# Attention of a two-layer kernel: weighted sum ahead of the row-minimum products, transposes back ahead of the output projection

## What is computed

```python
x = x + attention0(layernorm(x), ctx)      # rope on q and k
x = x + experts0(layernorm(x))             # top 2 of 8 experts + a shared one
x = x + attention1(layernorm(x), ctx)      # key mask, no rope
x = x + experts1(layernorm(x))             # top 4 of 16 experts + a shared one
# attention:
q, k, v = heads(x @ Wq.T + bq), heads(ctx @ Wk.T + bk), heads(ctx @ Wv.T + bv)
scores = einsum('bhsd,bhtd->bhst', q, k) / sqrt(16)
out = einsum('bhst,bhtd->bhsd', softmax(scores), v)
return out.reshape(B, S, 256) @ Wo.T + bo
```

## Time and profile before

| what | us |
|---|---|
| median of 3 runs | 952.73 (952.24 to 957.65) |
| profiled execution, time | 950.79 |
| profiled execution, span | 948.9 |
| TensorE busy | 868.0 (91% of the span) |
| VectorE busy | 650.6 (69%) |
| ScalarE busy | 483.4 (51%) |
| POOL busy | 383.0 (40%) |

### The profile page before, as it was taken

One profiled execution on the slowest core, in us unless ns is written; L12 is line 12 of the kernel. 1 busy time (PEld: TensorE's weight loads), 2 busy tenths in 40 slices (PEclk: granted clock), 3 DMA queues, 4 the chain that ended last, 5 costly groups with the idle time before them and its releaser, 6 DMA issues.

```text
span 948.9 us, 21025 instructions
## 1 busy us (share of the span) xinstructions
PE 868.0 (91%) x7941; PEld 763.1 (80%) x7941; DVE 650.6 (69%) x1364; ACT 483.4 (51%) x811; POOL 383.0 (40%) x389
## 2 busy tenths in 40 slices
PE   5689988889899999999777999899999999999997
PEld 4577766678899999999666788667788888888886
DVE  6868686675577777777575557559867666676676
ACT  3665669533367767676465665963222223223222
POOL 4354445057468888888513232301121131311210
PEclk9799999999999999999988999999999999999999
DMA  7019020014778888888530000100001010010002
GB/s 215 24 35 261 11 74 2 1 68 151 266 234 224 232 239 221 241 215 228 106 127 25 2 2 4 52 15 18 17 18 33 17 33 17 17 33 17 17 1 89
DMA packets 46176, 85.43 MB, mean 90 GB/s; under 512 B 6304, under 2 KB 33184, under 8 KB 45984
## 3 DMA queue, kind: packets, MB, share of 16 engines
q0 software_dynamic: 14784, 46.44, 17.8%
q1 hardware_dynamic: 31328, 38.09, 13.5%
HBM read 63.73 MB, written 20.79 MB: 89 GB/s over the span
## 4 chain that ended last, share of the span: by engine, by line
PE 64%; DVE 11%; ACT 9%; issue 6%; DMA 5%; POOL 4%; SPq 0%; DVEq 0%; ACTq 0%; POOLq 0%
PE bank L1430 35%; PE bank L1466 12%; PE bank L1525 4%; DMA w_raw<-in_fw,w_idx 2%; PE bank L1639 2%; ACT prob L760 2%; PE bank L1615 2%; PE bank L1689 2%; DVE low_f L1252 2%; PE bank L1723 2%; POOL summed L497 2%; DMA xs<-sorted_x 1%; DVE xres L1120 1%; PE bank L1699 1%; DVE xT_lo L943 1%
## 5 line engine op out<-in xcount | busy, mean ns | idle before, releaser
L1430 PE MATMUL bank<-xT_hi,w_hi 128*128 128x512 f32 x352 | 140.4, 399 | 2.8 <-DVE hid L1130 2.8
L691 ACT ACTIVATE act_sb<-bank 128x512 f32<-128x512 f32 x88 | 52.6, 598 | 172.3 <-PE bank L1430 172.3
L1430 PE MATMUL bank<-xT_lo,w_hi 128*128 128x512 f32 x352 | 140.1, 398 | 0.0
L1430 PE MATMUL bank<-xT_hi,w_lo 128*128 128x512 f32 x352 | 139.9, 397 | 0.0
L1130 DVE TENSOR_TENSOR hid<-bank,act_sb 128x512 f32<-128x512 f32 x88 | 60.9, 692 | 114.4 <-ACT act_sb L691 114.0
L1120 DVE SCALAR_TENSOR_TENSOR xres<-bank,gate,xres 128x256 f32<-128x256 f32 x320 | 132.6, 476 | 0.8 <-PE bank L1466 0.8
L427 POOL TENSOR_TENSOR w_hi<-w_raw,zero_col 128x768 fp32r<-128x768 f32 (+1 forms) x20 | 31.9, 1595 | 245.3 <-PE bank L1466 240.6
L1430 PE MATMUL bank<-xsT_hi,w_hi 128*128 128x256 f32 x368 | 106.4, 289 | 2.1 <-DVE xsT_lo L1094 1.5
L497 POOL DMA_INDIRECT summed<-y_sb,tile_to x46 | 96.4, 2096 | 25.2 <-issue 15.4
L1466 PE MATMUL bank<-w_hi,hid_hi 128*128 128x256 f32 x352 | 100.1, 284 | 5.8 <-DVE hid_lo L1135 5.8
L1430 PE MATMUL bank<-xsT_hi,w_lo 128*128 128x256 f32 x368 | 103.5, 281 | 0.0
(11 more groups left out here) (210 smaller groups left out, 2192.1 us busy)
## 6 DMA issues: line engine op xcount, KB each, us to landing
w_raw<-in_fw SPq DMA_DIRECT2D x18, 384.0 KB, 3.0
sorted_x<-empty_row SPq DMA_DIRECT2D x2, 2967.0 KB, 19.8
xs<-sorted_x SPq DMA_DIRECT2D x23, 258.0 KB, 3.3
ctx_raw<-in_ctxT SPq DMA_DIRECT2D x8, 512.0 KB, 4.5
xres<-in_x SPq DMA_DIRECT2D x4, 512.0 KB, 7.3
summed<-xres SPq DMA_DIRECT2D x4, 512.0 KB, 9.0
xres<-summed SPq DMA_DIRECT2D x4, 512.0 KB, 5.9
out_x<-xres SPq DMA_DIRECT2D x4, 512.0 KB, 3.0
```

Of the source, the lines that this page charges most:

```text
L691: nc.scalar.activation(act_sb[:, r, :], bank[2 * r + 1][:], ACT.Silu).then_inc(f["act"], 1)
L1430: last = nc.tensor.matmul(dst, lh, rh, start=(i == 0), stop=(i == len(pairs) - 1))
```

## The change

Three pairs of steps change places; no instruction's work is changed.

```diff
 # ScalarE, attend()
+                        if b >= 1:
+                            output_copy(b - 1)
                         exponential(b, 0)
                         exponential(b, 1)
-                        if b >= 1:
-                            output_copy(b - 1)
                         if b >= 2:
                             output_turned_copy(b - 2)
 # VectorE, attend()
+                        if b >= 1:
+                            output(b - 1)
                         if b >= 3:
                             residual(b - 3)
-                        if b >= 1:
-                            output(b - 1)
 # TensorE, attend()
                         if b >= 1:
                             scores_turned(b)
+                            weighed(b - 1)
                         lows_added(b)
                         if b == 0:
                             banks_read(1, X0)
                             banks_read(1, X1)
                             scores(1)
-                        if b >= 1:
-                            weighed(b - 1)
                         if b >= 2:
                             output_turned(b - 2)
+                        if b >= 1:
+                            turned_back(b - 1)
                         if b >= 3:
                             projected(b - 3)
-                        if b >= 1:
-                            turned_back(b - 1)
```

## The result

The changed kernel takes 963.49 us (median of 4 runs, 959.92 to 966.68) against 952.49 for the kernel before beside it: 1.0144 times as long, 95% interval 1.011 to 1.0179. A second set of runs gave 1.0142 (1.0115 to 1.0169). The forecast of 958.0 had the sign and about half of the size: 5.3 us of 11.0 in the first set and 12.5 in the second.

A forecast was written before the change was run, and what follows sets the result against it. TensorE's work was taken to bound item-filled blocks, and loops over the engines the item-free late ones. Seven terms summed to 5.35, say +5.3 us, on the 952.73 median: forecast 958.0 us, range 950 to 964.

The forecast's parts named there:

- 1 block 1 of layer 0: Block 1 of layer 0: copy, then table load, now precede the first exponential, which the first item needs; +1.1 us.
- 2 full blocks: Weighted sum newly waits for the first reduction, 0.13 us in some six blocks where TensorE never idles otherwise; +0.8 us.
- 3 other blocks with items: Blocks with items: last exponential about 0.65 us later, hidden except twice where scores waited for q_half; +0.25 us.
- 4 blocks 1 and 2 of layer 1: Layer 1: the transposes' 1.49 us wait goes, gaining 0.85; block 2 loses 0.65 again; -0.2 us.
- 5 block 12: Block 12 of each layer, bound by the output loop, gets shorter: -0.15 us together.
- 6 block 13: Block 13 of each layer: table load now stands behind the copy, loop 6.85 us instead of 6.29 before; +1.35 us.
- 7 blocks 14 and 15: Bound by exponentials: 5.57 us instead of 4.81 once per layer, and +0.35 until the last copy; +2.2 us.
- Clock: TensorE partly at 1.2 GHz after added idle time: an unknown price from 0 to +10 us, taken as 0.
- the clock's rival: Idle beyond about 1 us ahead of scores turned in blocks 13 to 15 lowers TensorE's clock: about 965 us; chance 0.10.
- aimed waits decide: TensorE's 9.2 us of waits for scaled output and copied weighted sum go, loads cost 2.45: 946 us; chance 0.15.
- Late exponentials in every block: Exponentials 0.65 us later cost time in some 20 blocks with items, 13 us on top: 971 us; chance 0.05.
- No difference: Late blocks gain as much as they lose: 952.7 us; chance 0.10.

The follow-up runs named there:

- stats_behind: Kernel before with VectorE's next_statistics of blocks 10 and 11 behind the output instead of ahead of the residual: 948.61 us, 0.9991 of the kernel before.
- sum_copy_only: Changed kernel with TensorE's projection ahead of the transposes back and VectorE's residual ahead of the output again: 960.01 us, 1.0131 of the kernel before.

## Why the prediction was wrong

By its own terms, with the changed kernel less before in block lengths, and blocks 1 and 2 of layer 0 held against 9.14 and 9.76 of `stats_behind`, where the clock had not fallen:

| term | forecast | measured |
|---|---|---|
| 1 block 1 of layer 0 | +1.1 | +1.3 (1.6 against 8.84) |
| 2 full blocks (3, 4, 8 of layer 0, 3 to 11 of layer 1) | +0.8 | +4.8 |
| 3 other blocks with items (2, 5, 6, 7, 9, 10, 11 of layer 0) | +0.25 | +1.1 |
| 4 blocks 1 and 2 of layer 1 | -0.2 | +0.1 |
| 5 block 12 | -0.15 | +0.7 |
| 6 block 13 | +1.35 | +1.85 |
| 7 blocks 14 and 15 | +2.2 | +2.6 |
| sum | +5.35 | +12.5 |

- The step that failed is term 2. It priced the new wait at 0.13 us in six blocks, and took the other orders as free where TensorE is full. Measured is 0.32 to 0.50 us in twelve blocks: in layer 1, 0.08 to 0.27 for the weighted sum's start (`sum_copy_only`), and 0.2 for the wait for the copy, a wait that the forecast did not have at all. Three errors stand behind it. I took a wait ahead of scores turned to cover the new one; it covers the reduction, but the weighted sum still starts 1.08 us after scores turned, where the lows' products started after 0.93. I gave the reduction no hand-over: in block 5 of layer 1 the first one, started at 544.95 and 0.68 long, ends at 545.63, and the weighted sum starts at 545.78, 0.15 later; that doubles the 0.13 of the forecast. And I counted the copy as 0.47, the distance to the next step of ScalarE, where the follower on another engine waits for its end, 0.60: by 0.47 the copy is ready 1.61 us after the weighted sum's start (1.08+0.06+0.47), just as TensorE arrives at 1.63 (540.10-538.75+0.28); measured, the transposes start at 1.79.
- The same errors are in term 5. The residual starts 0.11 after the projection's end and not 0.04, which rows 3 and 5 already showed (151.85-150.71-1.03), so 1.14 after the projection's first (542.17-541.03); the scores start 0.15 after the residual, a price that the sum did not have; the rest is the weighted sum's later start and the wait for the copy. Output loop of block 12 of layer 0, from the rows below: 2.14 to the weighted sum, 1.79 to the transposes, 0.49 to the projection, 1.14 + 0.42 + 0.15 through the residual = 6.13, and not 5.6. The residual as the new end of the loop was right, as the last bracket shows.

```profile
138.11 1.17 PE L1615 MATMUL bank<-k_full,q_half 32*128 32x128 f32 x32 [0.95 <-DVE xres L1268]
...
140.25 1.08 PE L1689 MATMUL bank<-prob,v_full 128*32 128x128 f32 x32
...
142.04 0.66 PE L1699 MATMUL bank<-ident,o_turned 128*128 128x128 f32 x4
142.53 1.03 PE L1723 MATMUL bank<-aw_out,oT 128*128 128x256 f32 x4
...
144.24 1.17 PE L1615 MATMUL bank<-k_full,q_half 32*128 32x128 f32 x32 [0.62 <-DVE xres L1268]
```

- Terms 1, 4, 6 and 7 were right in place and mechanism. The exponential loop is 5.72 instead of 5.57, since the weighted sum starts 1.08 after scores turned (153.51-152.43) and not 0.93; in block 13 it is 1.17 (146.38-145.21), and the load starts only with the copy's end, 0.62 after its start (148.13-147.51) and not 0.47, so 7.22 instead of 6.85. The load is on the path. The gain in block 1 of layer 1 came (0.68 of 0.85), and block 2 gave it back (0.81 of 0.65).
- Term 3: the q_half wait in block 6 cost 0.81 and block 7 gave 0.25 back, where I had written "most". The 0.65 itself should have been 0.61, 1.08-0.47.
- Clock: taken as 0. It did fall in the first profile, not late in the layers, where I had put it mostly, but in blocks 1 to 3 of layer 0. Late in a layer it stayed at 1.00, also in block 13 with TensorE's idle times of 0.48, 0.67 and 0.20, so nothing in these blocks bears out the condition on idle time that the clock's rival had. The clock explains part of the spread of the runs, not the difference: the trace without these falls is still 9.3 us longer than the profile of before, which had one.
- The rival "aimed waits decide" falls: the 5.1 us for o_sb went and the 4.1 for the copy shrank to 0.7, but others came, among them 2.2 us for the residual and 1.3 for oT ahead of the scores, and those that no bracket marks. "Late exponentials in every block" falls: ScalarE still idled 0.41 us ahead of the copy of the item. "No difference" falls with the ratio.

## What to carry to other kernels

An in-order engine's program that shows no gaps is a set of covers: before moving a step ahead, write down which wait each step hides, and price the hand-over by the end of the last instruction plus the latency that the trace shows, not by the distance at which the same engine goes on. A table load did best here directly behind the last user of the old table, ahead of the copy that waits for another engine. Where a reordering pays in single blocks, do it there alone, and compare loops by the distance between the same instruction in neighbouring blocks, at the same granted clock: it repeated to within 0.04 us in layer 1, where the run times of one kernel spread over 6 us.

## What the runs showed of the hardware

- A column-tiled product (128*32) behind row-tiled ones with a 32x256 right side started 1.08 us after their first, about at the end of the last; the 32*128 bf16 products behind the same group started after 0.87 to 0.93. It may be that these row-tiled products start while the earlier ones are still under way, and column-tiled ones do not; only the starts were measured.
- One execution of the same program had TensorE at 1.2 GHz for most of 50.2 to 54.9 us (granted 0.52) and of 65.0 to 68.6 us (0.53), another at 2.4 GHz in both. Ahead of the first stretch it had idled 2.15, 0.38 and 0.89 us:

```profile
46.44 1.08 PE L1689 MATMUL bank<-prob,v_full 128*32 128x128 f32 x32 [2.15 <-DVE low_f L1252]
...
48.23 1.11 PE L1699 MATMUL bank<-ident,o_turned 128*128 128x128 f32 x4 [0.38 <-ACT o_turned L765]
50.23 0.79 PE L1430 MATMUL bank<-xT_hi,aw_hi 128*128 128x512 f32 x1 [0.89 <-ACT prob L760]
```

The execution that stayed at 2.4 GHz had idled about as long at the same three places, 1.57, 0.37 and 1.34 us. What decides between the two was not settled.
